# x read by channel and weight halves formed from the raw weights, in the opening of an RWKV + MoE layer

## Chip, core and metric

The kernel runs on one core of one Trainium2 chip. The metric is the device time of one execution in microseconds (us). The engines are TensorE (PE, with its weight loads PEld), VectorE (DVE), ScalarE (ACT), GpSimd (POOL) and SyncE (SP), which here only issues transfers.

## The reference

The layer works on x of 2 sequences x 2048 steps x 256 channels, in float32:

```python
xx = jnp.pad(x, ((0, 0), (1, 0), (0, 0)))[:, :-1, :]      # x one step earlier
xk = x * time_mix_k + xx * (1.0 - time_mix_k)             # the same for xv, xr
k, v, r = xk @ Wk.T, xv @ Wv.T, xr @ Wr.T
rwkv = sigmoid(r) * wkv(time_decay, time_first, k, v)     # a scan over the 2048 steps
x = _layernorm(x + rwkv @ Wo.T)
logits = x @ Wg + bg                                      # top 2 of 8 experts, softmax of the two
y_e = act_e(x @ W1[e] + b1[e]) @ W2[e] + b2[e]            # act: gelu for even e, silu for odd e
x = _layernorm(x + sum of the two chosen y_e, weighted)
```

## The kernel before

**Two phases.** Phase A computes the attention part and the routing, phase B the experts. In phase A the 2048 steps of both sequences are cut into 8 chunks of 256 (`NCH` = 8), each 512 columns wide (2 sequences) and 2 blocks of 128 channels deep (`CC` = 2). Phase B works through blocks of 256 tokens of one expert. Every engine has its own program, and they meet by semaphores. In each program phase A is a function `step(i)`, called for i from -2 to 9, in which the stages of several chunks stand in an order written out by hand. On VectorE step i begins with the running maximum of chunk i (`stabilise`: four scans at L1225, two `nd` operations at L1232), then come the division of chunk i-1 (`divide`), the two long scans q and p of chunk i (L1289, L1291, in `accumulate`), `numerator`, the residual of chunk i-1, its statistics, the routing of chunk i-2, and the lower halves of chunk i+2.

**Halves.** The projections are made from an upper and a lower half of each operand: the upper half is the value copied to the type fp32r, the lower is what is left. For x they are `xh` (ScalarE, L1023) and `xl` (VectorE, L1301), for the weights `wq`. x comes in by rows of time (`xin`), and TensorE turns it with eight 128x128 transposes to each chunk (`transpose_x`, L696) into `xT_ps`, from which both halves are read. Since a projection also needs x one step earlier, `xh` and `xl` have a column ahead of the chunk, which is copied from the chunk before (L1020, L1298).

**Projections.** `project` (L705) makes 24 products of 512 columns to each of k, v and r of a chunk. k of chunk i+1 waits for `nd` of chunk i (same PSUM banks). r and v share two banks: r of a chunk waits until v of the chunk before has been copied out, v waits until the sigmoid of r (`gates`, ScalarE L1000) has read them.

**Opening.** SyncE issues x of chunk 0, five small transfers with the mixing factors and decay constants as rows (`const_rows`), then Wk, Wv and Wr. TensorE first runs products of ones (`idle_products`, L677), turns the constants (L682), turns x, and runs more of them. Each weight matrix is multiplied by the mixing factor and by one minus it (`scale_matrix`, L417; Wk on VectorE, Wv and Wr on GpSimd) into `wscaled`; ScalarE copies the upper half in one operation (L970), VectorE takes the lower in one (L1151). Only then does k of chunk 0 start. b1 is also turned on TensorE (L687).

**ScalarE in step i.** Exponents of chunk i (L984 to L994), sigmoids of chunk i+1 (a table load at L1057 first), upper halves of chunk i+2, logarithm and exponential for the inverse of the denominator (`inverse`, L1029, L1031, with tables of their own), the normalisation (L1038), and the copy of v of chunk i+1 (`copy_v`, L979). In step 0 the second half of v of chunk 0 is copied behind the exponents.

**GpSimd** splits the first expert's weights, computes the reciprocal deviations and sends the routed rows to DRAM (L611). **SyncE** loads chunk i+2 of x when its transposes of chunk i are done.

## Time and profile before

| | us |
|---|---|
| median of 3 runs | 688.1 (687.56 to 694.36) |
| the profiled execution's own time | 694.94 |
| its span | 693.0 |
| mean granted TensorE clock | 0.954 of full speed |
| busy: PE | 629.8 (91%) |
| busy: DVE | 459.1 (66%) |
| busy: ACT | 378.3 (55%) |
| busy: POOL | 334.1 (48%) |

The span runs from the first to the last instruction on the core; the execution's time has 1.9 us more around it. The profiled execution is one of the longer ones. Phase A fills about the first 250 us, phase B reaches to about 660, the rest is the final normalisation. Shares over the whole span are averages over these stages, so the views below are taken by stage.

### The profile page before, as it was taken

To read this page: it belongs to the slowest core of one execution; us is meant where nothing else is said; L and a number is where in the kernel's file an instruction comes from. 1 tells how busy PE (TensorE), PEld (TensorE's weight loads), DVE (VectorE), ACT (ScalarE), POOL (GpSimd) and SP (SyncE) were. 2 spreads that over 40 slices of the span, in tenths; PEclk is the share of its full clock that TensorE was granted. 3 is DMA by queue.
4 is the path that set the end of the run, shared out by engine and by line. 5 is a ranking of instruction groups with operands and counts; after the bars stand their busy time and mean duration, and the time that the engine had idled before them with its cause. 6 is when DMAs were issued, how large, how long until landed. Compare 5 with 4: busy or idle time off the path is not lost.

```text
span 693.0 us, 14687 instructions
## 1 busy us (share of the span) xinstructions
PE 629.8 (91%) x4555; PEld 581.2 (84%) x4555; DVE 459.1 (66%) x1051; ACT 378.3 (55%) x690; POOL 334.1 (48%) x322
## 2 busy tenths in 40 slices
PE   7999999999977778999999999999999999999900
PEld 5787888878864567999999999999999999999900
DVE  4879999999998565555646465566575565555334
ACT  3566685585765223646463636375564646464417
POOL 6112037546546768229257374357384366131335
PEclk9999999999989789999999999999999999999965
DMA  8610221421324645532633525323516322331267
GB/s 245 169 32 0 92 92 63 138 85 54 108 92 152 223 156 150 160 58 38 175 47 124 94 46 154 64 49 119 96 29 177 55 42 42 53 46 17 35 197 309
DMA packets 53309, 70.61 MB, mean 102 GB/s; under 512 B 5482, under 2 KB 46900, under 8 KB 53076
## 3 DMA queue, kind: packets, MB, share of 16 engines
q1 hardware_dynamic: 31012, 43.24, 19.0%
q0 software_dynamic: 13216, 17.09, 14.0%
q10 hardware_dynamic: 8976, 8.82, 4.8%
q8 instruction: 73, 1.20, 0.7%
q14 instruction: 32, 0.26, 0.1%
HBM read 40.86 MB, written 29.06 MB: 101 GB/s over the span
## 4 chain that ended last, share of the span: by engine, by line
PE 71%; DVE 11%; issue 6%; ACT 5%; DMA 3%; POOL 2%; SPq 0%; DVEq 0%; ACTq 0%; POOLq 0%
PE y_ps L884 27%; PE hT_ps L875 26%; PE vr_ps L705 6%; PE k_ps L705 5%; ACT zz L1137 2%; PE xT_ps L893 2%; PE wo_ps L713 2%; DVE o_all L1225 2%; POOL records_dram L611 2%; PE small_ps L727 1%; DMA recs<-records_dram 1%; DVE xl L1301 1%; PE xT_ps L775 1%; PE xT_ps L696 1%; DVE nd L1232 1%
## 5 line engine op out<-in xcount | busy, mean ns | idle before, releaser
L875 PE MATMUL hT_ps<-xTh,wx 128*128 128x256 f32 x1120 | 208.2, 284 | 3.0 <-DVE aTl L1195 2.7
L649 POOL DMA_INDIRECT x_dram<-y_sb,dest x70 | 108.6, 1551 | 195.2 <-DVE y_sb L1212 117.7
L884 PE MATMUL y_ps<-wx,aTh 128*128 128x256 f32 x1088 | 190.9, 279 | 2.3 <-DVE y_sb L1212 2.3
L875 PEld LDWEIGHTS hT_ps<-xTh,wx 128*128 128x128 f32 x1120 | 175.5, 190 | 3.6 <-DVE aTl L1195 3.6
L1195 DVE TENSOR_TENSOR aTl<-hT_ps,aTh 128x512 fp32r<-128x512 f32 x140 | 93.5, 689 | 123.0 <-ACT aTh L1098 120.8
L884 PEld LDWEIGHTS y_ps<-wx,aTh 128*128 128x128 f32 x1088 | 165.4, 189 | 2.7 <-issue 2.7
L875 PE MATMUL hT_ps<-xTl,wx 128*128 128x256 f32 x560 | 157.3, 281 | 0.0
L884 PE MATMUL y_ps<-wx,aTl 128*128 128x256 f32 x544 | 151.7, 279 | 0.0
L1092 ACT ACT_TABLE_LOAD x33 | 42.3, 1283 | 161.4 <-PE hT_ps L875 159.8
L1092 ACT ACTIVATE hT_ps<-hT_ps,b_c 128x256 f32<-128x256 f32 x280 | 113.7, 469 | 23.7 <-PE hT_ps L875 21.1
L611 POOL DMA_INDIRECT records_dram<-rec,slot_i x64 | 77.4, 1209 | 64.7 <-DVE slot_i L1351 34.1
L875 PEld LDWEIGHTS hT_ps<-xTl,wx 128*128 128x128 f32 x560 | 106.5, 190 | 0.0
L884 PEld LDWEIGHTS y_ps<-wx,aTl 128*128 128x128 f32 x544 | 102.1, 188 | 0.0
L705 PE MATMUL vr_ps<-xh,wq 128*128 128x512 f32 x256 | 87.1, 412 | 0.1
L1098 ACT ACTIVATE aTh<-hT_ps 128x512 fp32r<-128x512 f32 x140 | 84.3, 648 | 0.0
L555 POOL TENSOR_TENSOR wx<-staging,wx 128x512 fp32r<-128x512 f32 x56 | 70.3, 1292 | 0.6
L705 PEld LDWEIGHTS vr_ps<-xh,wq 128*128 128x128 f32 x256 | 49.8, 195 | 12.1 <-ACT v L979 0.6
L1210 DVE TENSOR_TENSOR y_ps<-y_ps,b_b 128x256 f32<-128x256 f32 x70 | 30.1, 431 | 43.0 <-DVE weight L1191 19.6
L705 PE MATMUL vr_ps<-xl,wq 128*128 128x512 f32 x128 | 51.9, 405 | 0.0
L705 PE MATMUL k_ps<-xh,wq 128*128 128x512 f32 x128 | 42.3, 401 | 3.1 <-DVE nd L1232 2.1
L1212 DVE TENSOR_SCALAR y_sb<-y_ps,weight 128x256 f32<-128x256 f32 x70 | 33.9, 484 | 2.5
L705 PEld LDWEIGHTS k_ps<-xh,wq 128*128 128x128 f32 x128 | 24.2, 189 | 9.7 <-issue 4.1
(198 smaller groups left out, 845.3 us busy)
## 6 DMA issues: line engine op xcount, KB each, us to landing
staging<-in_L_ffn_W SPq DMA_DIRECT2D x16, 1024.0 KB
recs<-records_dram ACTq DMA_DIRECT2D x33, 261.0 KB, 3.4
xin<-in_L_attn_x SPq DMA_DIRECT2D x16, 256.0 KB, 4.3
xres<-in_L_attn_x SPq DMA_DIRECT2D x16, 256.0 KB, 3.2
x_dram<-rec SPq DMA_DIRECT2D x16, 256.0 KB, 3.4
zz<-x_dram SPq DMA_DIRECT2D x8, 512.0 KB, 7.6
out<-zz SPq DMA_DIRECT2D x8, 512.0 KB, 4.4
records_dram<-pad_rec SPq DMA_DIRECT2D x8, 261.0 KB, 3.9
```

The source lines that it names most:

```text
L555: pool.tensor_tensor(wx[:, e % 2, 1, at], raw[:, at], wx[:, e % 2, 0, at].bitcast(F32), ALU.subtract).then_inc(weights_ready if n == LOWER ...
L611: pool.indirect_dma_start(xs, bass.IndirectOffsetOnAxis(ap=slot_i[at][:, n:n + 1], axis=0), rec[at][:, j, :], None, bounds_check=DUMMY - 1 ...
L649: pool.indirect_dma_start(sums, bass.IndirectOffsetOnAxis(ap=dest[t.slot][:, h:h + 1], axis=0), y_sb[t.slot][:, h, :], None, bounds_check= ...
L705: ins = pe.matmul(out_ps.rearrange("p (b t) -> p b t", b=B), wq[:, mat, now, part, cc, oc * P:(oc + 1) * P], xpart[c.slot][:, cc, :, now:n ...
L713: ins = pe.matmul(wo_bank(c, b)[:, h, :], mixed[:, cc, b, h * P:(h + 1) * P], wo[:, cc, :], start=cc == 0, stop=cc == CC - 1)
L875: ins = pe.matmul(hT_ps[b][:, f, :], wx[:, s, part, off:off + P], xpart[t.slot % 2][:, cc, :], start=k == 0, stop=k == len(terms) - 1)
L884: ins = pe.matmul(y_ps[h], apart[t.slot % 2][:, fc, h * P:(h + 1) * P], wx[:, s, part, off:off + C], start=k == 0, stop=k == len(terms) - 1)
L1092: act.activation(hT_ps[b][:, f, :], hT_ps[b][:, f, :], func, bias=b1_c[:, bass.ds(expert * FC + (2 * b + f), 1)]).then_inc(act_done, 1)
L1098: act.activation(aTh[u.slot % 2][:, 2 * b - 2:2 * b, :], hT_ps[b - 1][:], ACT.Copy).then_inc(aTh_done, 1)
L1195: dve.tensor_tensor(aTl[u.slot % 2][:, 2 * b:2 * b + 2, :], hT_ps[b][:], aTh[u.slot % 2][:, 2 * b:2 * b + 2, :].bitcast(F32), ALU.subtract ...
L1210: dve.tensor_tensor(y_ps[h], y_ps[h], b2_b[:, bass.ds(expert * C, C)], ALU.add).then_inc(bias_added, 1)
L1212: dve.tensor_scalar(y_sb[u.slot][:, h, :], y_ps[h], weight[u.slot][:, h:h + 1], None, ALU.mult).then_inc(y_done, 1)
```

## The change

**Layouts.** x is also handed over with channels as rows (`x_by_channel`), the mixing factors, decay and first as one 128x10 array of columns, b1 as 128x64 columns. These arrays exist before the launch. `xt` takes the place of `xin`; the transposes of x, of the constants and of b1 fall away. Each load of `xt` brings the column of one step earlier with it (257 columns), so the two small copies fall away, and from chunk 1 on each half of x is one operation of 128x1028 (in chunk 0 one to each channel block).

**Weights' halves.** ScalarE forms the upper half straight from the raw weights, four operations of 128x256 to each matrix with the factor as the per-partition scale; VectorE forms the lower with `scalar_tensor_tensor`, four to each matrix. `scale_matrix` falls away.

**Order.** x of chunk 0 is issued on ScalarE's own queue. TensorE begins with 16 products of ones in a row. In step 0 ScalarE copies v before the exponents, and takes the upper halves of chunk 2 and the inverse ahead of the sigmoids of chunk 1, with two more table loads.

```diff
+        def load_turned(sp, c):
+            skip = 1 if c.number == 0 else 0
+            for b in range(B):
+                sp.dma_start(xt[c.slot][:, :, b, skip:TC + 1],
+                             xT[b].rearrange("(c p) t -> p c t", p=P)[:, :, c.number * TC - 1 + skip:(c.number + 1) * TC]).then_inc(xt_in[c.slot], 16)
...
-            load_chunk(sp, xin[0], x, plain(0), xin_in[0])
-            for n, row in enumerate([m.rearrange("a b (c p) -> (a b c) p", p=P) for m in (mix_k, mix_v, mix_r)] +
-                                    [v.rearrange("(c p) -> c p", p=P) for v in (decay, first)]):
-                sp.dma_start(const_rows[n * CC:(n + 1) * CC, :], row).then_inc(consts_in, 16)
+            sp.dma_start(consts_c[:], columns).then_inc(consts_in, 16)
             load_matrix(0, wkT)
             load_matrix(1, wvT)
             load_matrix(2, wrT)
+            load_turned(sp, plain(1))
...
-                    sp.wait_ge(xT_done, (c - 2).upto(CC))
-                    load_chunk(sp, xin[c.slot], x, c, xin_in[c.slot])
+                    sp.wait_ge(xl_done, (c - 2).upto(1))
+                    load_turned(sp, c)
...
-            idle_products(6, vr_ps[0][:])
-            pe.wait_ge(consts_in, 5 * 16)
-            pe.transpose(small_ps[:, 256:256 + 5 * CC], const_rows[:], ident[0:5 * CC, 0:5 * CC]).then_inc(consts_turned, 1)
+            idle_products(16, vr_ps[0][:])
...
+                    if c.number == 0 and mat == 0 and oc == 0 and n % (len(terms) // CC) == 0:
+                        pe.wait_ge(w_lo, 2 * (cc + 1))
+                        pe.wait_ge(*((first_xl, cc + 1) if cc < CC - 1 else (xl_done, 1)))
...
-                    if (i + 2).exists:
-                        transpose_x(i + 2)
...
             def upper_weights(n):
-                act.wait_ge(scaled[n], 2 * CC)
-                act.activation(wq[:, n, :, 0, :, :], wscaled_of(n), ACT.Copy).then_inc(w_hi, 1)
+                if n == 0:
+                    act.wait_ge(setup_dve, 1)
+                act.wait_ge(weights_in[n], 16)
+                for cc, a, factor in parts():
+                    act.activation(wq[:, n, a, 0, cc, :], raw_matrix(n, cc), ACT.Identity,
+                                   scale=factor[:, n, cc:cc + 1]).then_inc(w_hi, 1)
...
                 if i.exists:
-                    exponents(i)
                     if i.number == 0:
                         copy_v(i, 1)
+                    exponents(i)
...
-                if (i + 1).exists and i.number >= 0:
+                if i.number == 0:
+                    upper_halves(i + 2)
+                    inverse(i)
+                    act.preload_act_table(ACT.Sigmoid)
                     gates(i + 1)
-                    act.preload_act_table(ACT.Ln)
-                if (i + 2).exists and i.number >= 0:
-                    upper_halves(i + 2)
-                if i.exists:
+                    act.preload_act_table(ACT.Exp)
+                elif i.exists:
+                    if (i + 1).exists:
+                        gates(i + 1)
+                        act.preload_act_table(ACT.Ln)
+                    if (i + 2).exists:
+                        upper_halves(i + 2)
                     inverse(i)
...
             def lower_halves(c):
...
+                rows = lambda a: a[:].rearrange("p c b t -> p (c b) t")[:, :, 0:TC + 1]
+                dve.tensor_tensor(rows(xl[c.slot]), rows(xt[c.slot]), rows(xh[c.slot]).bitcast(F32), ALU.subtract).then_inc(xl_done, 1)
```

ScalarE, from the first instruction to v of chunk 0. Before:

```order
L966 ACT_TABLE_LOAD
L966 ACTIVATE consts_c<-consts_c 128x2
L970 ACTIVATE wq<-num 128x2x512
L1023 ACTIVATE xh<-xT_ps 128x2x256 x2
L970 ACTIVATE wq<-den 128x2x512
L970 ACTIVATE wq<-r 128x2x512
L1020 ACTIVATE xh<-xh 128x4
L1023 ACTIVATE xh<-xT_ps 128x2x256 x2
L979 ACTIVATE v<-vr_ps 128x512
```

And with the change (`nd` is where Wk lies at first):

```order
L378 DMA xt<-in_x_by_channel 128x2x256 x2
L936 ACT_TABLE_LOAD
L936 ACTIVATE consts_c<-consts_c 128x2
L943 ACTIVATE wq<-nd,unmix_c 128x256
L943 ACTIVATE wq<-nd,consts_c 128x256
L943 ACTIVATE wq<-nd,unmix_c 128x256
L943 ACTIVATE wq<-nd,consts_c 128x256
L996 ACTIVATE xh<-xt 128x2x257 x2
```

The one long copy is now four short operations on the raw matrix, and the engine also issues the loads of x. The eight operations for Wv and Wr follow behind `xh`.

ScalarE in step 0, from the exponents of chunk 0 to the copy of v of chunk 1. Before:

```order
L989 ACTIVATE A<-A 128x4x256
L979 ACTIVATE v<-vr_ps 128x512
L994 ACTIVATE bonus<-nd,consts_c 128x512 x2
L1057 ACT_TABLE_LOAD
L1000 ACTIVATE gate<-vr_ps 128x512 x4
L1064 ACT_TABLE_LOAD
L1020 ACTIVATE xh<-xh 128x4
L1023 ACTIVATE xh<-xT_ps 128x2x256 x2
L1029 ACTIVATE r<-den 128x1024
L1031 ACT_TABLE_LOAD
L1031 ACTIVATE r<-r 128x1024
L979 ACTIVATE v<-vr_ps 128x512 x2
```

And with the change:

```order
L963 ACTIVATE A<-A 128x4x256
L968 ACTIVATE bonus<-nd,consts_c 128x512 x2
L1033 ACT_TABLE_LOAD
L974 ACTIVATE gate<-vr_ps 128x512 x2
L999 ACTIVATE xh<-xt 128x4x257
L1005 ACT_TABLE_LOAD
L1005 ACTIVATE r<-den 128x1024
L1007 ACT_TABLE_LOAD
L1007 ACTIVATE r<-r 128x1024
L1042 ACT_TABLE_LOAD
L974 ACTIVATE gate<-vr_ps 128x512 x2
L1044 ACT_TABLE_LOAD
```

The sigmoids of chunk 1 (the third and fourth `gate`) moved behind the inverse of chunk 0, between two table loads that were not there.

TensorE at the start. Before:

```order
L677 MATMUL vr_ps<-ones_h 128x512 x6
L682 MATMUL small_ps<-ident,const_rows 128x10
L696 MATMUL xT_ps<-ident,xin 128x128 x8
L677 MATMUL vr_ps<-ones_h 128x512 x4
L687 MATMUL small_ps<-ident,b_rows 128x64
L677 MATMUL vr_ps<-ones_h 128x512 x5
```

And with the change:

```order
L667 MATMUL vr_ps<-ones_h 128x512 x16
L681 MATMUL k_ps<-xh,wq 128x512
L681 MATMUL k_ps<-xl,wq 128x512
L681 MATMUL k_ps<-xh,wq 128x512 x2
L681 MATMUL k_ps<-xl,wq 128x512
```

Fifteen products of ones with transposes between them became sixteen in a row.

## Rows read from the trace of the kernel before

**Rows 1.** Windows by stage: times, busy us (instructions) by engine, PEclk, DMA share, GB/s

```profile
115.00:117.00 2.00, 2.00 (x6) 1.51 (x6) 1.90 (x8) 1.98 (x3) 1.74 (x4) 0.50 0.32 115
117.30:143.20 25.90, 25.90 (x136) 21.41 (x135) 24.96 (x56) 16.78 (x26) 14.42 (x17) 1.00 0.31 103
193.60:265.60 72.00, 51.92 (x308) 41.19 (x307) 52.36 (x169) 31.14 (x55) 44.00 (x48) 0.81 0.47 155
265.60:660.00 394.40, 389.98 (x3348) 388.98 (x3347) 222.78 (x473) 208.80 (x433) 199.47 (x132) 1.00 0.38 80
```

**Rows 2.** Chain of waits that ended last: start us, us, what

```profile
3.40 2.77 DMA nd<-in_L_attn_Wk
69.68 5.88 PE k_ps L705 x24
83.79 1.73 PE wo_ps L713 x8
87.73 0.94 PE xT_ps L696 x8
103.34 5.67 PE vr_ps L705 x24
113.89 7.18 PE vr_ps L705 x24
169.19 1.44 DVE o_all L1225 x3
```

**Rows 3.** Timeline of TensorE, opening: start us, us, engine, line, operation, count [idle before]

```profile
2.46 2.74 PE L677 MATMUL vr_ps<-ones_h 128*128 128x512 bf16 x6 [2.46 <-POOL lane L534]
7.09 1.60 PE L677 MATMUL vr_ps<-ones_h 128*128 128x512 bf16 x4
8.83 1.25 PE L677 MATMUL vr_ps<-ones_h 128*128 128x512 bf16 x5
11.10 0.47 PE L705 MATMUL k_ps<-xh,wq 128*128 128x512 f32 x1 [1.02 <-DVE xl L1301]
```

**Rows 4.** Transfers of the first 12 us: KB each, median us to landing

```profile
xin<-in_L_attn_x SPq DMA_DIRECT2D x4, 256.0 KB, 3.2
```

**Rows 5.** Timeline of ScalarE, phase A

```profile
18.04 1.07 ACT L1023 ACTIVATE xh<-xT_ps 128x512 fp32r<-128x512 f32 x2
44.96 1.28 ACT L1031 ACT_TABLE_LOAD   x1
46.25 1.06 ACT L1031 ACTIVATE r<-r 128x1024 f32<-128x1024 f32 x1
47.22 1.07 ACT L979 ACTIVATE v<-vr_ps 128x512 f32<-128x512 f32 x2
93.10 2.06 ACT L1038 ACTIVATE rec<-xres,shift,rstd 128x256 f32<-128x256 f32 x4
```

**Rows 6.** Timeline of VectorE, phase A

```profile
26.57 1.23 DVE L1285 TENSOR_TENSOR b2v<-B,v 128x1024 f32<-128x1024 f32 x1 [3.23 <-ACT v L979]
47.34 1.23 DVE L1246 TENSOR_TENSOR newton<-den,r 128x1024 f32<-128x1024 f32 x1 [1.96 <-ACT r L1031]
52.35 2.29 DVE L1289 TENSOR_TENSOR_SCAN q_all<-A,B 128x1028 f32<-128x1028 f32 x1
66.23 2.66 DVE L1225 TENSOR_TENSOR_SCAN o_all<-w_row,o_all,k_ps 128x256 f32<-128x256 f32 x4
91.39 2.66 DVE L1225 TENSOR_TENSOR_SCAN o_all<-w_row,o_all,k_ps 128x256 f32<-128x256 f32 x4
111.35 0.68 DVE L1363 TENSOR_TENSOR xres<-wo_ps,xres 128x512 f32<-128x512 f32 x1
115.49 0.17 DVE L1298 CAST xl<-xl 128x4 fp32r<-128x4 f32 x1
115.57 1.28 DVE L1301 TENSOR_TENSOR xl<-xT_ps,xh 128x512 fp32r<-128x512 f32 x2
117.23 2.66 DVE L1225 TENSOR_TENSOR_SCAN o_all<-w_row,o_all,k_ps 128x256 f32<-128x256 f32 x4 [0.30 <-DVE o_all L1220]
```

More of the change, by code:

```diff
@@ L81, in upto, with build @@
         return self.m * (self.every * each) + (self.off * each + n)
-def build(nc, x, decay, first, mix_k, mix_v, mix_r, wkT, wvT, wrT, woT, w1, b1, w2, b2, wgT, bg, out):
+def build(nc, x, wkT, wvT, wrT, woT, w1, w2, b2, wgT, bg, xT, columns, b1_columns, out):
     B, T, C = x.shape
@@ L193, in build @@
         rec = [sb(f"rec{n}", [P, J, REC], F32, phase_a) for n in range(RECS)]
-        xin = [sb(f"xin{n}", [P, B, TH, C], F32, phase_a) for n in range(2)]
+        xt = [sb(f"xt{n}", [P, CC, B, TC + 2], F32, phase_a) for n in range(2)]
         xres = [sb(f"xres{n}", [P, B, TH, C], F32, phase_a) for n in range(2)]
@@ L1141, in _ @@
         def _(dve):
[L1142 to L1144 removed]
+            dve.wait_ge(consts_in, 16)
             dve.tensor_scalar(unmix_c[:], mix_c, -1.0, 1.0, ALU.mult, ALU.add).then_inc(setup_dve, 1)
[L1146 to L1147 removed]
+            dve.memset(A2[:, :, :, 0:1], 0.0).then_inc(setup_dve, 1)
+            dve.memset(seen[:], 0.0).then_inc(setup_dve, 1)
+            dve.wait_ge(setup_act, 1)
+            dve.tensor_scalar(decay_c, decay_c, -1.0, None, ALU.mult).then_inc(setup_dve, 1)
+            dve.wait_ge(setup_dve, 4)
+            dve.tensor_tensor(first_c, first_c, decay_c, ALU.add).then_inc(setup_dve, 1)
+            for cc in range(CC):
+                dve.tensor_copy(w_row[:, cc, :], decay_c[:, cc:cc + 1].broadcast_to([P, TC])).then_inc(setup_dve, 1)
             def lower_weights(n):
[L1150 to L1153 removed]
+                for part, (cc, a, factor) in enumerate(parts()):
+                    dve.wait_ge(w_hi, 2 * CC * n + part + 1)
+                    dve.scalar_tensor_tensor(out=wq[:, n, a, 1, cc, :], in0=raw_matrix(n, cc), scalar=factor[:, n, cc:cc + 1],
+                                             in1=wq[:, n, a, 0, cc, :].bitcast(F32), op0=ALU.mult, op1=ALU.subtract).then_inc(w_lo, 1)
             def finish_setup():
@@ L1157, in finish_setup @@
                 lower_weights(2)
[L1158 to L1166 removed]
+                dve.wait_ge(setup_dve, 5 + CC)
                 dve.wait_ge(made2, 9)
[L1168 to L1169 removed]
             def halves(u):
@@ L1498 @@
     arrays, aps = {}, []
-    for name in INPUTS:
-        a = np.asarray(inputs[name])
-        a = np.ascontiguousarray(a.T if name in TRANSPOSED else a)
+    given = {name: np.asarray(a) for name, a in inputs.items()}
+    laid_out = {name: given[name].T if name in TRANSPOSED else given[name] for name in INPUTS}
+    laid_out["x_by_channel"] = given["L0_attn_x"].transpose(0, 2, 1)
+    laid_out["columns"] = np.concatenate([given[name].reshape(-1, P) for name in COLUMNS]).T
+    laid_out["b1_columns"] = given["L0_ffn_b1"].reshape(-1, P).T
+    for name, a in laid_out.items():
+        a = np.ascontiguousarray(a)
         arrays[f"in_{name}"] = a
```

130 lines of the change are left out of this document (41 added, 89 removed).

## The prediction

> **What bounds the kernel now.** I read the windows by stage first, then the chain of waits, then the timelines of TensorE, ScalarE and VectorE in phase A. Phase B is TensorE alone, busy 389.98 of 394.40 us [rows 1]; the change puts nothing there and takes nothing away, so I cost it at nothing. In phase A two engines are almost equally full: in the window from 117.30 TensorE is busy for all of its 25.90 us and VectorE for 24.96 [rows 1]. So work taken from TensorE alone pays only as far as VectorE allows. The opening is a serial chain that nothing hides: the landing of Wk (issued at 3.40, landed at 6.17 [rows 2]), scaling, upper and lower half, halves of x, and k of chunk 0 at 11.10, with TensorE idle for 1.02 us before it [rows 3].
>
> The sum below is made against the profiled execution, span 693.0 and own time 694.94 us. That is 6.8 us above the median of 688.1; two of the four executions known lie near 694 and two near 688.
>
> **Opening (until k of chunk 0).** SyncE no longer issues x and five small transfers ahead of Wk, only the columns, so Wk is issued at about 1.2 in place of 3.40. At its old landing time of 2.77 it would be there at 4.0 [rows 2]. It now shares the transfer engines with x of chunk 0, issued on the other queue at 0.8; a 256 KB transfer of x took 3.2 in the median [rows 4]. I take 4.4 for Wk and 5.3 for x. ScalarE then makes four upper halves of 128x256 in place of one copy. The nearest row is four operations of that size in 2.06 [rows 5], so they end at 6.5; the two upper halves of x take 1.07 [rows 5], and half of that, then one lower half of 128x514 on VectorE (1.28 for two [rows 6]) gives 6.5 + 0.55 + 0.65 + small gaps = 7.8. The four lower halves of Wk run one behind ScalarE's and are done by 7.0. The halves of Wv and Wr (eight more operations, some 4.2 us on ScalarE by the same row) end at about 11.7, behind k's 5.9 us, so they are hidden; without that cover they would cost up to 2.1 to each matrix.
>
> But TensorE's 16 products of ones stand ahead of k. At the low of the two clock levels six of them took 2.74, 0.43 each from the second on, and later, at the high one, five took 1.25 [rows 3]. From 2.46 all sixteen at 1.2 GHz last until 9.3. In the execution before, four products from 7.09 still took 1.60, the five from 8.83 were fast [rows 3]; with a rise at about 8.6 here too they end at 9.0. If the clock rises three us earlier, they end at about 7.4, and the data at 7.8 decide. No row shows which. I take 8.4, the middle. **Opening: 11.10 - 8.4 = 2.7 us, between 1.8 and 3.3.**
>
> **Steps 0 and 1.** k, v and r take 5.6 to 5.9 us each (k 5.88, r 5.67 [rows 2]). From k of chunk 0 TensorE works without a pause until v of chunk 1, whose copy at 47.22 releases ScalarE's exponents [rows 5] and these the scan q at 52.35 [rows 6]. Two groups of eight transposes stood in that stretch, 0.94 each by the chain's piece at 87.73 [rows 2]: 1.9 us. For this to count, VectorE and ScalarE must keep up. Today VectorE waits 3.23 us for v of chunk 0 at 26.57 and 1.96 for the inverse at 47.34 [rows 6]. The first wait shrinks: v is copied ahead of the exponents. In its place b2v waits for the exponents themselves, which start when v's second half is out (8.4 + 5.9 + 5.7 + 0.6 for the copy = 20.6) and are ready three operations of about 1.0 later, at 23.6, 2.97 before today's 26.57. The second goes: the inverse is ready at about 34 (worked out below), and VectorE, which reached it at 45.4 and waited [rows 6], reaches the division at about 39. What is late next is the copy of v of chunk 1, as before: v ends at 47.2 - 2.7 - 1.9 = 42.6, and q starts at about 47.7 in place of 52.35. VectorE then idles some 3.6 us ahead of b2v, off the path. The larger halves `xh` of chunk 1 to 7 cost no more than today's two pieces (1.07). Behind q, the product with the gate meets the sigmoid of chunk 2 about 0.2 late. **Steps 0 and 1: 1.9 - 0.2 = 1.7 us.** The first scan of step 2, at 66.23 before, comes at about 61.8.
>
> The moved order adds two table loads to ScalarE's step 0. A load took 1.28, and the exponential behind it began 1.29 after the load did [rows 5]. So inverse and sigmoids of chunk 1 line up as: `xh` 29.4, load and logarithm 31.7, load and exponential 34.1, load 35.4, first sigmoid 36.0. TensorE wants to start v of chunk 1 at 37.1 and finds its bank free: the loads lie in the shadow of r. The Trainium skill, ScalarE: Activation LUTs, section What ACT_TABLE_LOAD costs, speaks against this: each switch of set costs a drain of about 1.38 us on top of the load. The trace does not agree, since nothing of that length stands behind the load in the rows. By that page the first sigmoid would end three drains later, and the sum would be smaller by the amount given among the rivals.
>
> **Steps 2 to 5.** Each loses its eight transposes on TensorE (0.94), one small copy on each of ScalarE and VectorE, and two lower halves become one. VectorE sets the pace now. Step 3 lasts 117.23 - 91.39 = 25.84 us and holds 0.30 of waiting [rows 6]; the rest, 25.54, is VectorE's own. The small copy goes (the next operation starts 0.08 after it), and one operation of 128x1028 in place of two (1.28 [rows 6]) should take as long as b2v's 128x1024, 1.23 [rows 6]: 25.4 remain. Step 2 (25.16) has no waiting for x, and wins only 0.13. Step 3 wins 0.43, and steps 4 and 5, 169.19 - 117.23 = 51.96 [rows 2, 6], win 1.15. In step 6 no halves are made, and it stays. **Steps 2 to 5: 1.7 us.** TensorE's other 0.6 us a step turn into idle time before k. Bounds: 0.5, if the waits above VectorE's own pace came only from the low clock in this execution (a window at 0.50 [rows 1], v of a chunk 7.18 in place of 5.67 [rows 2]); 2.5, if VectorE's small gaps close too.
>
> **What costs nothing.** GpSimd loses `scale_matrix` in the opening; its next work waits for the first expert's weights anyway. SyncE's loads of x now wait for VectorE's lower halves of two chunks back and come many us early. b1 comes in as it is used. The rest of phase A and the tail are only shifted.
>
> **Sum.** 2.7 + 1.7 + 1.7 = 6.1 us of 694.94 gives 688.8 for an execution like the profiled one. Against the median of 688.1 I take off 5.6, since part of the 1.7 in steps 2 to 5 is what the low clock cost there: **682.5 us**, 0.8% less.
>
> **The rivals.**
> - *The spread of the runs.* Executions near 694 and near 688 both occur, and the stretch from 193.60 to 265.60 has a granted clock of 0.81 [rows 1], so its length can vary. If the new median is one of the longer ones: 694.6 - 6.1 = 688.5. Two of the four executions known speak for it; against it, two of the three runs that make the median before were short.
> - *The opening is given back.* x by channel is read in pieces 8 KB apart. If they land 3 us late, k starts at 10.8 and the gain is 5.6 - 2.4: 684.9. Against it: every transfer of that piece length lands in about 3 us [rows 4]. If also the first clock rise is late, no more is lost, since it lies beside.
> - *Table loads with a drain.* Three drains end the first sigmoid of chunk 1 at 40.1, 3.0 after TensorE wants v: 682.5 + 3.0 = 685.5. This is the page's rule as a mechanism; the rows speak against it.
> - *More than the sum.* If the transposes also caused the low clock in steps 3 and 5, and the later start of the tail falls well, up to 4 us more come: 678.5. For it: the slow v follows directly on the routing products and the transposes.
> - *Slower.* TensorE now stands idle before every k from step 2 on, 1.3 to 1.7 us a step. If that brings its clock down for k and what follows until the second half of the out-projection, the chain that ends at 83.79 + 1.73 [rows 2], this lies on VectorE's path: the residual there is due at 111.35, 19.96 us into its step, and the chain takes 85.52 - 66.23 = 19.29 [rows 2, 6], slack 0.67. One stretch at the low clock costs 7.18 - 5.67 = 1.5 [rows 2], two a step 3.0, less the slack 2.3, over four steps 9.3: 682.5 + 9.3 = 691.8, slower than before. It decides from 2.1 us of lost time a step. Against it: an idle of 1.02 before k in the opening is followed by k products at full pace.
>
> **Chances.** Forecast 0.52 (its own range 679.5 to 685), spread 0.14, opening given back 0.09, drains 0.03, more than the sum 0.15, slower 0.07. That the change does not do what it says is not open here. About 1% is what a measurement can tell from no change, 681.2 and 695.0. Of the forecast's case about 0.4 lies below 681.2, since the bounds of the opening (0.6) and of the steps (0.8) both leave room there; with the case of more, faster is 0.52 x 0.4 + 0.15 = 0.36. Slower by over 1% needs the low clock before k and the longer runs together: 0.04. Same: 0.60. The range of 678.5 to 689 leaves out 0.2, the slower case and edges of others.
>
> **What would show it.** k of chunk 0 starting at 7.8 to 9.3; scan q of chunk 1 at about 47.7; steps 2 to 5 of 25.0, then 25.4 us; TensorE idle for over 1 us before each k; no idle on TensorE before v of chunk 1. A start of k after 10, a wait of v of chunk 1 for `gates`, or steps above 25.8 would make the prediction wrong.

## The result and the profile after

The changed kernel takes 687.28 us in the median of 20 runs (683.97 to 689.82), the kernel before 691.94 in the median of 20 (687.56 to 694.97): ratio 0.9936, 95% interval 0.9919 to 0.9953. The medians are 4.7 us apart; by the ratio the gain is 4.4 us (3.3 to 5.6). Forecast were 682.5 us and, against the 688.1 shown then, 5.6 us less, a ratio of 0.9919. The profiled execution of the changed kernel has a span of 688.0 and an own time of 689.71, where the one before had 693.0 and 694.94.

The windows by stage of the changed kernel, which answer to [rows 1] (step 3 starts 5.5 us earlier here, and its low clock lies elsewhere in the step); the columns are as there:

```profile
115.00:117.00 2.00, 1.81 (x8) 1.53 (x9) 1.97 (x4) 1.27 (x2) 0.00 (x0) 1.00 0.91 305
111.70:137.20 25.50, 24.67 (x121) 20.11 (x120) 24.81 (x55) 17.52 (x24) 14.78 (x15) 0.94 0.32 104
187.00:265.60 78.60, 61.47 (x359) 49.62 (x358) 56.35 (x176) 33.01 (x59) 50.04 (x53) 0.78 0.50 162
265.60:655.00 389.40, 384.15 (x3297) 383.31 (x3295) 220.08 (x466) 206.80 (x429) 194.09 (x128) 1.00 0.38 78
```

VectorE is now busy for 24.81 of a step of 25.50 us, and TensorE for 24.67, with pauses of its own. Next the chain of waits (start us, us, what), for [rows 2]:

```profile
2.45 6.34 PE vr_ps L667 x16
8.79 5.68 PE k_ps L681 x24
48.39 1.73 PE wo_ps L689 x8
82.92 7.27 PE vr_ps L681 x24
98.77 5.69 PE vr_ps L681 x24
162.69 1.44 DVE o_all L1203 x3
```

The chain now opens with the sixteen products of ones (`vr_ps L667`) in place of the landing of Wk. One v still takes 7.27 us where others take 5.7. The timeline of TensorE, for [rows 3], and its waits before a later k (in brackets the idle time and what ended it):

```profile
2.45 6.34 PE L667 MATMUL vr_ps<-ones_h 128*128 128x512 bf16 x16 [2.45 <-POOL lane L528]
8.56 0.47 PE L681 MATMUL k_ps<-xh,wq 128*128 128x512 f32 x1
64.89 0.47 PE L681 MATMUL k_ps<-xh,wq 128*128 128x512 f32 x1 [1.70 <-DVE nd L1210]
115.19 0.47 PE L681 MATMUL k_ps<-xh,wq 128*128 128x512 f32 x1 [0.83 <-DVE nd L1210]
166.14 0.47 PE L681 MATMUL k_ps<-xh,wq 128*128 128x512 f32 x1 [1.37 <-DVE nd L1210]
```

k of chunk 0 starts at 8.56 in place of 11.10. Transfers of the first 12 us (KB each, median us to landing), for [rows 4]:

```profile
xt<-in_x_by_channel ACTq DMA_DIRECT2D x2, 256.0 KB, 4.3
nd<-in_L_attn_Wk SPq DMA_DIRECT2D x1, 256.0 KB, 4.1
```

ScalarE, for [rows 5]: the last of the four upper halves of Wk, the first of the exponents of chunk 0, then inverse and sigmoid in their new order, and the second copy of v of chunk 1:

```profile
6.67 0.49 ACT L943 ACTIVATE wq<-nd,consts_c 128x256 fp32r<-128x256 f32 x1
20.68 1.05 ACT L958 ACTIVATE B<-nd 128x1024 f32<-128x1024 f32 x1
29.17 1.28 ACT L1005 ACT_TABLE_LOAD   x1
30.46 1.06 ACT L1005 ACTIVATE r<-den 128x1024 f32<-128x1024 f32 x1
31.55 1.28 ACT L1007 ACT_TABLE_LOAD   x1
32.84 1.06 ACT L1007 ACTIVATE r<-r 128x1024 f32<-128x1024 f32 x1
33.92 1.28 ACT L1042 ACT_TABLE_LOAD   x1
35.21 0.60 ACT L974 ACTIVATE gate<-vr_ps 128x512 f32<-128x512 f32 x1
42.75 0.60 ACT L953 ACTIVATE v<-vr_ps 128x512 f32<-128x512 f32 x1 [2.22 <-PE vr_ps L681]
```

VectorE, for [rows 6]: the lower halves of x of chunk 0, `b2v` and q of chunk 1, the single lower half of a chunk, and the first scans of steps 2 to 7:

```profile
7.72 1.30 DVE L1275 TENSOR_TENSOR xl<-xt,xh 128x514 fp32r<-128x514 f32 x2
46.22 1.23 DVE L1263 TENSOR_TENSOR b2v<-B,v 128x1024 f32<-128x1024 f32 x1 [3.06 <-ACT B L961]
47.36 2.30 DVE L1267 TENSOR_TENSOR_SCAN q_all<-A,B 128x1028 f32<-128x1028 f32 x1
61.45 2.66 DVE L1203 TENSOR_TENSOR_SCAN o_all<-w_row,o_all,k_ps 128x256 f32<-128x256 f32 x4
86.25 2.66 DVE L1203 TENSOR_TENSOR_SCAN o_all<-w_row,o_all,k_ps 128x256 f32<-128x256 f32 x4
110.39 1.23 DVE L1281 TENSOR_TENSOR xl<-xt,xh 128x1028 fp32r<-128x1028 f32 x1
111.74 2.66 DVE L1203 TENSOR_TENSOR_SCAN o_all<-w_row,o_all,k_ps 128x256 f32<-128x256 f32 x4
137.21 2.66 DVE L1203 TENSOR_TENSOR_SCAN o_all<-w_row,o_all,k_ps 128x256 f32<-128x256 f32 x4
162.69 2.66 DVE L1203 TENSOR_TENSOR_SCAN o_all<-w_row,o_all,k_ps 128x256 f32<-128x256 f32 x4
187.06 2.66 DVE L1203 TENSOR_TENSOR_SCAN o_all<-w_row,o_all,k_ps 128x256 f32<-128x256 f32 x4
```

The steps last 24.8, then 25.49, 25.47, 25.48 and 24.37 us. Behind phase A lies phase B, which begins with the first product of hT. The timeline of TensorE shows it at 248.11 in the kernel before and at 241.75 in the changed one, 6.36 us earlier:

```profile
248.11 0.55 PE L875 MATMUL hT_ps<-xTh,wx 128*128 128x256 f32 x1
```
```profile
241.75 0.55 PE L844 MATMUL hT_ps<-xTh,wx 128*128 128x256 f32 x1
```

The last stage begins with the last scatter of results. The chain of waits there, in the kernel before and in the changed one:

```profile
660.87 3.64 DMA x_dram<-y_sb,dest
665.63 3.65 DMA zz<-x_dram
672.99 12.90 ACT zz L1137 x26
```
```profile
654.15 3.61 DMA x_dram<-y_sb,dest
658.88 5.38 DMA zz<-x_dram
667.98 12.39 ACT zz L1121 x25
```

From the last scatter to the end the kernel before takes 693.0 - 660.87 = 32.1 us, the changed one 688.0 - 654.15 = 33.8. The first eighth of the rows lands 3.65 us after its issue in the one, 5.38 in the other.

The account of the two profiled executions: start of step 7, 193.58 to 187.06, 6.52 less; from there to phase B 54.53 and 54.69; phase B to the last scatter 412.76 and 412.40; last stage 1.72 more. 6.52 - 0.16 + 0.36 - 1.72 = 5.0, the difference of the spans. Single profiles of one kernel differ too (the kernel before starts step 7 between 192.56 and 193.58 in its three profiles), so this account is repeated below with means of three.

### The profile page after: what moved, and what is told of

Read it like the earlier page. It is cut to its first block, busy times and chain, and to the rows that moved or that the text cites. A ratio compares the mean times of both kernels' runs of the same rounds, so it can differ in the third digit from the quotient of the medians.

```text
span 688.0 us, 14522 instructions
## 1 busy us (share of the span) xinstructions
PE 626.3 (91%) x4490; PEld 576.9 (84%) x4490; DVE 458.8 (67%) x1040; ACT 382.7 (56%) x687; POOL 330.3 (48%) x313
## 3 DMA queue, kind: packets, MB, share of 16 engines
HBM read 40.88 MB, written 29.06 MB: 102 GB/s over the span
## 4 chain that ended last, share of the span: by engine, by line
PE 72%; DVE 12%; issue 6%; ACT 3%; DMA 3%; POOL 3%; DVEq 0%; ACTq 0%; SPq 0%; POOLq 0%
PE hT_ps L844 27%; PE y_ps L853 27%; PE vr_ps L681 7%; PE k_ps L681 4%; ACT zz L1121 2%; PE xT_ps L862 2%; POOL records_dram L601 2%; DVE o_all L1203 2%; PE wo_ps L689 1%; DMA recs<-records_dram 1%; DVE stats L1300 1%; PE vr_ps L667 1%; PE small_ps L703 1%; DMA zz<-x_dram 1%; DVE newton L1231 1%
## 5 line engine op out<-in xcount | busy, mean ns | idle before, releaser
L601 POOL DMA_INDIRECT records_dram<-rec,slot_i x64 | 75.1, 1174 | 65.7 <-DVE slot_i L1330 34.8
L689 PE MATMUL wo_ps<-wo,newton 128*128 128x256 f32 x112 | 29.5, 411 | 4.2 <-DVE newton L1231 4.2
```

What stands on the lines that cost most here:

```text
L601: pool.indirect_dma_start(xs, bass.IndirectOffsetOnAxis(ap=slot_i[at][:, n:n + 1], axis=0), rec[at][:, j, :], None, bounds_check=DUMMY - 1 ...
L689: ins = pe.matmul(wo_bank(c, b)[:, h, :], mixed[:, cc, b, h * P:(h + 1) * P], wo[:, cc, :], start=cc == 0, stop=cc == CC - 1)
```

## The experiments

Each kernel was run several times beside the kernel before on the same chip; four chips served in these runs, on which the kernel before has medians of 692.0, 694.2 (693.9 in a second group of runs), 696.3 and 697.7 us. Ratios are to the kernel before, with 95% intervals. Three questions stand behind them: which part of the change gives what in phase A; where the rest of the forecast is; and what TensorE's clock does in the tail of phase A, the stretch from step 7 to hT. The letters that the expectations give to their theories are explained there. This table has all runs (starts in us, from each profile; "last stage" is from the last scatter to the end):

| run | ratio | k of chunk 0 | q of chunk 1 | step 7 | hT | last stage |
|---|---|---|---|---|---|---|
| kernel before | | 11.10 | 52.35 | 193.58 | 248.11 | 32.1 |
| before again (2nd) | 1.0009 (0.9986 to 1.0031) | 11.14 | 52.02 | 192.56 | 246.83 | 31.3 |
| before again (3rd) | 0.9998 (0.9974 to 1.0021) | 11.15 | 52.02 | 193.10 | 248.34 | 31.9 |
| changed | 0.9936 (0.9919 to 0.9953) | 8.56 | 47.36 | 187.06 | 241.75 | 33.8 |
| changed again (2nd) | 0.9938 (0.9911 to 0.9964) | 8.30 | 47.10 | 186.82 | 241.07 | 33.8 |
| changed again (3rd) | 0.9928 (0.9904 to 0.9953) | 8.38 | 47.30 | 187.01 | 242.96 | 32.9 |
| step 0 in the old order | 0.9943 (0.9917 to 0.9969) | 8.46 | 48.90 | 188.16 | 242.0 | 33.3 |
| before, x by channel only | 1.0018 (0.9998 to 1.0037) | 11.29 | 51.97 | 191.22 | 245.49 | 33.2 |
| before, second copy unused | 0.9985 (0.9967 to 1.0003) | 11.12 | 51.99 | 193.15 | 248.18 | 32.5 |
| changed, copy declared last | 0.9929 (0.9902 to 0.9956) | 7.71 | 46.51 | 186.23 | 242.16 | 33.2 |
| changed, transposes back | 0.9928 (0.9904 to 0.9952) | 7.93 | 48.48 | 189.10 | 244.07 | 33.5 |
| changed, gate on GpSimd | 0.9925 (0.9899 to 0.9952) | 8.43 | 47.34 | 185.95 | 241.34 | 33.7 |
| changed, spare rows | 0.9928 (0.9904 to 0.9953) | 8.01 | 46.81 | 186.51 | 240.63 | 33.8 |
| before, spare rows | 1.0005 (0.9982 to 1.0027) | 11.06 | 51.95 | 192.44 | 246.54 | 31.6 |
| changed, 8 idle products | 0.9868 (0.9835 to 0.9900) | 8.48 | 47.28 | 186.97 | 238.22 | 33.0 |
| before, 8 idle products | 0.9955 (0.9934 to 0.9976) | 11.15 | 52.35 | 193.90 | 244.66 | 33.4 |
| changed, opening late | 0.9956 (0.9934 to 0.9979) | 11.71 | 50.63 | 190.35 | 246.51 | 33.7 |
| changed, 14 idle products | 0.9930 (0.9906 to 0.9954) | 8.29 | 47.08 | 186.83 | 245.20 | 33.1 |
| changed, 8 again | 0.9941 (0.9916 to 0.9965) | 8.53 | 47.33 | 187.08 | 241.64 | 34.8 |
| changed, 4 idle products | 0.9935 (0.9910 to 0.9960) | 8.56 | 47.48 | 187.21 | 243.77 | 35.1 |

### Both kernels again

> The kernel before, unchanged, profiled a second time. Theory T (phase A gained what was forecast, and the rest of the program gave some back by chance): its step 7 begins between 192.0 and 193.6 us, and from there to the last scatter of phase B it differs from the first profile's 467.3 us by up to 3 us either way. Theory L (the first profile was a lucky or unlucky one in phase A): its step 7 begins more than 1.5 us away from 193.6. Time: same as before, 692 us within 1.

> The changed kernel, unchanged, profiled a second time. Theory T: k of chunk 0 starts at 8.4 to 9.0, step 7 at 187.1 within 0.8; the final stage, from the last scatter on, takes 32.1 us as in the kernel before and not 33.9 again. Theory P (the second copy of x in memory slows the last loads and stores): the final stage takes 33.9 again. Time 687.3 within 1.

The gain repeats: 0.9938 after 0.9936, and 1.0009 for the kernel before against itself. So a ratio of this size is resolved, and differences of a quarter of a per cent between two edited kernels are not. Step 7 of the kernel before starts at 192.56, as theory T has it. The last stage of the changed kernel takes 33.8 us again, which theory P expected and theory T did not.

### Step 0 in the old order

```diff
+                    exponents(i)
                     if i.number == 0:
                         copy_v(i, 1)
-                    exponents(i)
...
-                if i.number == 0:
-                    upper_halves(i + 2)
-                    inverse(i)
-                    act.preload_act_table(ACT.Sigmoid)
-                    gates(i + 1)
-                    act.preload_act_table(ACT.Exp)
```

> The changed kernel with ScalarE's old order in step 0: the exponents before the copy of v, the sigmoids of chunk 1 before the upper halves and the inverse, two table loads fewer. If the order matters as in the forecast (VectorE waited for the inverse), scan q of chunk 1 comes later by up to 1 us, since VectorE would reach the division at 39 and the inverse be ready at about 42: the division ends at about 46.5, b2v's partner is ready at 46.2, so 0.3 to 1.5 us slower. Rival (the order is idle, PE's chain through v of chunk 1 sets q anyway): no change within 0.5 us.

q of chunk 1 starts at 48.90, 1.5 to 1.8 us later than in the changed kernel's three profiles, and step 7 1.1 to 1.3 later. ScalarE then comes to the copies of v too late, as its timeline in this kernel shows (43.77 for both, behind the inverse, where the changed kernel copied the second half at 42.75):

```profile
41.51 1.28 ACT L1007 ACT_TABLE_LOAD   x1
42.80 1.06 ACT L1007 ACTIVATE r<-r 128x1024 f32<-128x1024 f32 x1
43.77 1.07 ACT L953 ACTIVATE v<-vr_ps 128x512 f32<-128x512 f32 x2
```

So the moved order is worth a good microsecond in the profile; in the timed runs 0.9943 against 0.9938 shows no difference, and intervals of half a per cent could not show one of that size.

### Before, with x by channel only

```diff
-            load_chunk(sp, xin[0], x, plain(0), xin_in[0])
+            load_turned(sp, plain(0))
...
-                    transpose_x(i + 2)
-                    idle_products(4, vr_ps[0][:])
+                    idle_products(8, vr_ps[0][:])
```

> The kernel before with x by channel alone: no transposes of x, constants and weights as before, k of chunk 0 about where it was, at 11. Theory of the forecast: it gains the 1.7 us of steps 0 and 1 less what the old order in step 0 keeps (0 to 1), and the 1.1 to 1.7 of steps 2 to 5, so step 7 begins 2 to 3.4 us before 193.6 and the time is 688.5 to 690. Rival (the opening is all of the gain): step 7 begins within 1 us of the kernel before and the time is 691 to 692.

The ratio is 1.0018 (0.9998 to 1.0037), where 2 to 3.5 us less were expected: this part alone wins nothing that the time shows. k of chunk 0 waits for its data as before (the timeline of TensorE), because the scaling of Wk still stands ahead of it:

```profile
11.29 0.47 PE L701 MATMUL k_ps<-xh,wq 128*128 128x512 f32 x1 [1.14 <-DVE xl L1291]
```

q of chunk 1 stays at 51.97 although sixteen transposes are gone: without the new order VectorE and ScalarE hold it. Only steps 2 to 6 shorten, 191.22 - 65.61 = 125.61 against 193.58 - 66.23 = 127.35 (126.67 and 127.21 in the two other profiles of the kernel before, so by 1.1 to 1.7), and the last stage is longer by 1 to 2 us. Step 7 comes 1.3 to 2.4 us earlier than in those three profiles, and none of it arrives in the time.

### The second copy of x in memory

In the kernel before, x by channel is declared and 4 KB of it read; in the changed kernel, it is declared behind the output.

```diff
+            sp.dma_start(spare[:], xT[0, 0:P, 0:8]).then_inc(spare_in, 16)
```
```diff
+    result = nc.dram_tensor("out", shape, F32, kind="ExternalOutput").ap()
```

> The kernel before, with x by channel handed over as a further array that is not used (one 4 KB read of it in the opening, no engine waits for it). Theory P (the mere presence of a further 4 MB array moves what the final stage reads, and makes that slower): the first load of the final stage takes 4.9 to 6.7 us in place of 3.6, the stretch from the last scatter to the end 33.2 to 33.9 in place of 31.3 to 32.1, and the time rises by about 1.7 us over the kernel before. Rival (what the kernel reads matters, not what lies there): 3.6, 31.3 to 32.1, and the same time.

> The changed kernel with x by channel declared behind the output array. Theory P, if the order of declaration decides where the arrays lie: the first load of the final stage takes 3.6 us again, the final stage 31.3 to 32.1, and the time is 1.7 us below the changed kernel. If it does not decide: no change. Rival: no change.

0.9985 and 0.9929: neither the presence of the array nor its place in the list shows a cost in time. The last stages are 32.5 and 33.2 us. That the place in the list moves the array in memory isn't shown, so theory P gets no support here, but is not excluded either. In the profile with the unused copy the chain waits for a load that landed 6.92 us after its issue, although nothing is read by channel but 4 KB: such late landings are not the changed kernel's alone.

### The transposes' work put back

```diff
+                        for j in range(J):
+                            pe.transpose(xT_ps[:, cc, j * P:(j + 1) * P], ident[:], ident[:])
```

> The changed kernel with eight transposes of the identity where the transposes of x stood (none of them waited for, in the opening one group behind k of chunk 0). Theory of the forecast (TensorE's share was worth 1.7 us in steps 0 and 1 and, since VectorE then sets the pace, 1.1 to 1.7 in steps 2 to 5): step 7 begins at about 190 in place of 187, scan q of chunk 1 at 49.1, steps 3 to 5 take 25.7 to 25.9, and the time rises by 3 us. Rival (steps 2 to 5 are VectorE's alone): steps 3 to 5 stay at 25.5 and step 7 begins at 189.

k of chunk 0 starts at 7.93 and q of chunk 1 at 48.48, 40.55 apart, where the changed kernel has 38.80 and the kernel before 41.25 (40.88 and 40.87 in its other profiles). Put back, the two groups of transposes cost 1.75 us in steps 0 and 1. Put beside the run with x by channel only, 51.97 - 11.29 = 40.68, this shows that neither part does it alone: the transposes taken out win 0.2 to 0.6 us here, the new order 0.3 to 0.7, both together 2.0 to 2.5. Steps 2 to 6 take 189.10 - 62.57 = 126.53 against 125.61, so 0.9 there. The timed ratio, 0.9928, doesn't show these 2.7 us (0.4%), where 3 us were expected. Its interval is half a per cent wide; the six runs lie between 687.71 and 690.74 us, those of the changed kernel with the copy declared last between 687.14 and 691.20.

### The gate's product on GpSimd

```diff
-                dve.tensor_tensor(num[:], num[:], gate[i.slot][:], ALU.mult).then_inc(gated_done, 1)
+                    pool.tensor_tensor(num[:], num[:], gate[i.slot][:], ALU.mult).then_inc(gated_done, 1)
```

> The changed kernel with the product with the gate (1.14 us of VectorE's path in each chunk) moved to GpSimd. Theory (VectorE is the bound in steps 2 to 6): these steps shorten, each until TensorE's about 24.7, so by 0.7 to 1.1 us, step 7 begins 4 to 6 us earlier and the time falls by as much. Rival (TensorE or the chain through both engines still bounds): steps stay at 25.5. Third way: GpSimd is slower on it than VectorE's slack (2.6 us or more) or slows VectorE on the same memory port, and the division waits: steps longer than 25.5.

1.2 us taken from VectorE in each step bring step 7 forward by only 1.1 us (185.95), where 4 to 6 were expected; all of it is won in steps 2 to 6, since step 2 starts at 61.43 as before. These steps take 24.8, 25.8, 24.8, 25.4 and 23.7. Only steps 4 and 6 are shorter than in the changed kernel (25.5 and 24.4 there), and in both TensorE had pauses: in windows at their bounds it was busy for 24.64 and 23.00 us. In steps 3 and 5 of the changed kernel it was busy for all of the 25.5 us, VectorE for 24.8, and there less work on VectorE wins nothing. Both engines are nearly full, as the prediction read it in [rows 1].

### The place of the row results in memory

```diff
-    xs = nc.dram_tensor("records_dram", (DUMMY + BLK, REC), F32, kind="Internal").ap()
+    xs = nc.dram_tensor("records_dram", (DUMMY + BLK + B * T, REC), F32, kind="Internal").ap()
```

> The changed kernel, with 4 MB of unused rows added to the records' array in device memory, so that the array of row results behind it may lie elsewhere; no instruction changes. So far the stage from the last scatter to the end took 33.2 to 33.9 us in every kernel that reads x by channel, and 31.3 to 32.5 us in three profiles of kernels that don't. If the place of the row results in memory sets that (theory A), this kernel's last stage moves, to 31.3 to 32.5 us, and the time drops by about 1.5 us against the changed kernel (ratio to the kernel before 0.991). If it is something that the change does to the last stage itself, or the change's own arrays do by being read (theory B), it stays at 33.2 to 33.9 us (ratio 0.993). Phase A as in the changed kernel in both: first scan of step 7 at 186.5 to 187.5 us.

> The kernel before, with the same 4 MB of unused rows added to the records' array. Theory A (place in memory): the last stage may move to 33.2 to 33.9 us, and the time rises by about 1.5 us (ratio 1.002). Theory B: it stays at 31.3 to 32.5 us (ratio 1.000). If it comes to over 33 us here although nothing is read by channel, theory B falls; if both kernels with the spare rows stay as they are, theory A falls. Phase A as before: first scan of step 7 at 192.5 to 193.6 us.

Neither kernel's last stage moves: 33.8 and 31.6 us. Nothing supports theory A, though no row shows that the array of row results did move.

### The opening made late

```diff
-            idle_products(16, vr_ps[0][:])
+            idle_products(32, vr_ps[0][:])
```

> The changed kernel with 32 idle products in the opening instead of 16, so that the first k product comes at 14.6 to 14.9 us instead of 8.5 and every later step of phase A about 6.2 us later, at the times of the kernel before. If a microsecond of phase A is a microsecond of the whole (theory E), the time rises by 6.2 us against the changed kernel (ratio to the kernel before 1.0015 to 1.003), and the last stage stays at 33.2 to 33.9 us. If the last stage and the stretch behind the last scan step are shorter when everything is later (theory F: the kernel before gets back there what it lost), the last stage falls to 31.3 to 32.5 us and the ratio comes to 0.999 to 1.000.

The dose was half of what I had worked out: the sixteen more took 9.62 - 6.34 = 3.3 us, 0.21 each, as the timeline of TensorE in this kernel shows.

```profile
2.45 9.62 PE L667 MATMUL vr_ps<-ones_h 128*128 128x512 bf16 x32 [2.45 <-POOL lane L528]
11.71 0.58 PE L681 MATMUL k_ps<-xh,wq 128*128 128x512 f32 x1
```

k of chunk 0 and step 7 both come 3.3 us later than in the third profile of the changed kernel on the same chip (11.71 and 8.38; 190.35 and 187.01). The medians are 694.32 and 691.11, 3.2 us apart; the ratios 0.9956 and 0.9928 make it 2.0, with intervals that overlap. This fits theory E, a microsecond of the whole for each microsecond of the opening, but does not measure it closely. The last stage doesn't get shorter (33.7), so with this dose nothing is seen of theory F.

### A third profile of both, for the last stage

> The kernel before once more, for its last stage: 32.13 and 31.27 us in its two profiles so far. If the difference of the last stage between the two kernels is real, it comes to 31.2 to 32.5 us again (ratio 1.000); if it is chance, it may as well come to over 33 us, as in the kernel before with idle products (33.35 us).

> The changed kernel once more, for its last stage: 33.85 and 33.84 us in its two profiles so far, with the first load landing 5.4 us after its issue. Real difference: 33.2 to 33.9 us again; chance: anything from 31.3 us on. Ratio to the kernel before 0.993 to 0.994; phase A as in its other profiles (first scan of step 7 at 186.8 to 187.1 us).

Ratios 0.9998 and 0.9928. The load that the last stage waits for, in the chains of the kernel before (the first load) and of the changed one (here the second, issued 0.4 us behind the first):

```profile
666.32 3.50 DMA zz<-x_dram
```
```profile
660.06 6.21 DMA zz<-x_dram
```

Last stages of 31.9 and 32.9 us, the second below the 33.2 that a real difference was expected to give. In this profile of the changed kernel the first load was not late: VectorE starts on its rows at 663.52, 3.9 us after its issue. Over three profiles each the kernel before has 32.1, 31.3 and 31.9, the changed one 33.8, 33.8 and 32.9. The two don't overlap, and the mean difference is 1.8 us; of the edited kernels before, those with x by channel and with idle products have 33.2 and 33.4.

### Idle products in the tail of phase A

```diff
                             turn_early(0)
+                            idle_products(8, k_ps[:, 1, :])
```

> The changed kernel, with 8 idle products more in each step behind the last scan step, where the granted clock fell to half in its profile (226.8 to 247.3 us). If the clock in the tail of phase A is what TensorE's work there waits for (theory C: it also sets the spread of the runs, 684 us at a mean clock of 0.956 and 690 at 0.947), the clock stays high, the tail from the first scan of step 7 to the first y product drops from 77.3 to 79.3 us by 3 to 6 us, and the ratio to the kernel before comes to 0.985 to 0.990. If the products only add work (theory D), the tail is 1 to 3 us longer and the ratio 0.994 to 0.998.

> The kernel before, with the same 8 idle products in each step behind the last scan step. Its tail took 78.1 to 79.2 us in three profiles. Theory C (the clock in the tail decides): 3 to 6 us less, ratio 0.991 to 0.996, as much as for the changed kernel, since the tail is the same work in both. Theory D: ratio 1.001 to 1.004. If the products help one kernel and not the other, the tail isn't the same in both, and the forecast's part that the rest is only shifted fails there as well.

> The candidate for the best version, with two edits: 14 idle products instead of 8 behind the first turned half in each step behind the last scan step, and 12 instead of 16 in the opening. Theory C (TensorE's granted clock in the tail decides): the clock stays high through more of the tail, the ratio to the kernel before comes to 0.980 to 0.986. If 8 were enough already, or more of them only stand in front of the work, 0.987 to 0.991. The opening gives at most 0.7 us (first k product at 7.7 to 8.4 us, set by the data).

> The changed kernel with 8 idle products more in each step behind the last scan step, once more. Their first run gave 0.987 against the kernel before, 0.7% better than the changed kernel; 14 of them gave 0.993, no better than it. If 8 are right and 14 too many (theory C with a price: each costs its 0.21 us in front of the work), this run gives 0.985 to 0.989, and the first hT product comes at 238 to 240 us with a granted clock above 0.9 from 236 us on. If the first run was chance, the ratio comes to 0.991 to 0.995 and the first hT product at 241 to 243 us.

> The same with 4 idle products. Theory C with a price: half of the effect or all of it (0.985 to 0.991), since 4 cost only 0.8 us in front of the work of each step. If only the sum of work in the right place counts, and 8 was chance, 0.992 to 0.995 as in the changed kernel.

On the first chip 8 products helped both kernels: 0.9868, where the changed kernel with spare rows had 0.9928 on the same chip, and 0.9955 for the kernel before. hT began at 238.22. Windows of that run (times, busy us by engine, PEclk, DMA share, GB/s), then of its repeat on another chip, show what differs:

```profile
236.00:252.00 16.00, 13.42 (x107) 11.82 (x106) 12.75 (x48) 9.08 (x21) 10.86 (x12) 0.93 0.47 171
```
```profile
224.00:232.00 8.00, 5.59 (x32) 3.52 (x33) 4.56 (x29) 2.80 (x7) 5.64 (x9) 0.59 0.37 130
232.00:240.00 8.00, 4.58 (x37) 3.03 (x35) 3.88 (x24) 0.77 (x3) 6.05 (x7) 1.00 0.87 269
240.00:248.00 8.00, 6.58 (x35) 6.58 (x36) 4.88 (x20) 2.96 (x6) 4.09 (x4) 0.57 0.40 135
```

In the repeat the same program has the low level, 1.2 GHz, through much of 240 to 248, hT starts at 241.64, and the ratio is 0.9941. With 14 it is 0.9930, hT as late as 245.20 (that run has a second edit, 12 products in the opening in place of 16); with 4 it is 0.9935. The low stretch of the changed kernel's own profile is this window,

```profile
226.80:247.30 20.50, 17.17 (x81) 14.01 (x81) 11.51 (x57) 5.69 (x11) 12.99 (x18) 0.51 0.55 175
```

and in it the sixteen small products of the routing take 3.58 us where they take 1.95 at the high level. So the clock has a price in the tail. But it doesn't set the start of hT by itself, as TensorE's timeline in the run with 14 products shows:

```profile
236.59 1.95 PE L703 MATMUL small_ps<-wg,x1T 128*128 128x8 f32 x16
244.22 0.21 PE L776 MATMUL small_ps<-picks,before_h 128*128 128x32 bf16 x1 [4.36 <-DVE picks L1251]
```

Here the routing products run at the high level and end at 238.5, and then VectorE, which has nothing else to do, starts the first operation on their result only at 242.39, after an idle of 4.51 us for which the profile names no engine ("remote"). Such idles of 1 to 4.5 us, ahead of this operation or of the one that reads the counts made from it (`rank`), stand in the tail of the repeat with 8 products (1.24, 2.59 and 1.85), of the run with 4 (2.66 and 3.34), of the third profile of the changed kernel (2.12 and 3.39) and of all three of the kernel before; in the one good run with 8, and in the first two profiles of the changed kernel, there is none. What causes them is open. So for theory C a price of the clock is shown, on these products, but not what it is worth in the whole. As a remedy the idle products fail: they did not bring the gain a second time. No version was shown to be faster than the changed kernel on more than one chip.

## Why the prediction was right and wrong

**What failed: the level, first.** The step that failed is the base of the sum: "Against the median of 688.1 I take off 5.6". That median came from 3 runs, and two of the four executions known lay near 694. Over 20 runs the kernel before has 691.94. This base is 3.84 of the 4.78 us between 682.5 and 687.28. For an execution like the profiled one the same sum gave 688.8, and the profiled execution of the changed kernel took 689.71. The rival "the spread of the runs", at 0.14, gave this mechanism; it put the base at 694.6 and the time at 688.5, too high by 1.2. The measured ratio is safe from this, since both kernels were run side by side.

**What failed second: "the rest of phase A and the tail are only shifted."** The last stage was put at nothing and takes 1.8 us more (31.8 and 33.5 in the means of three profiles each). Up to hT the sentence held: step 7 comes 6.1 us earlier (193.08 and 186.96), and the way from there to hT takes 54.7 and 55.0. Phase B up to the last scatter takes 413.0 and 411.8; it was costed at nothing too, and gives 1.2 back, about as much as two profiles of the changed kernel differ (1.3). Together, 6.1 - 0.3 + 1.2 - 1.8 = 5.3 us in the profiles, forecast 6.1; 4.4 in the timed runs, forecast 5.6. In the last stage SyncE issues the same eight loads of 512 KB, and ScalarE's 32 operations take 15.8 us in both; what differs is how late the load on the chain lands. None of the experiments shows a cause: not the second copy's presence or its place in the list, not the added rows ahead of the row results, not an opening that starts 3.3 us later. Reading x by channel is not needed for a long last stage either: the kernel before with 8 idle products has 33.4 us. The cause stays open.

**What the timed runs do not show.** The shares below are read from profiles. Of the timed gain, only the opening's share has support from timed runs (3.2 us in the medians for 3.3 of delay). Taking out the transposes alone gave 1.0018, and putting their work back left 0.9928. So that the gain in steps 0 to 5 arrives in the time is argued from the account of the spans, not shown.

**Opening: right, in part by luck.** Forecast 8.4 (2.7 us), measured 8.56, 8.3 and 8.38, 2.7 in the mean. The parts differ: Wk and x took 4.1 and 4.3 us to land, and Wk, forecast for 4.4, let ScalarE start on its halves only at 5.46. The lower half of x's first block was there at about 7.72 + 0.65 = 8.4, not 7.8, and the products of ones ended beside it. 8.4 was the middle between two cases. In the second profile the products of ones took 5.07 us and ended at 7.5, and TensorE waited 0.79 us for the lower half; in the first and third they took 6.3 and TensorE did not wait.

**Steps 0 and 1: right, a little too low.** q of chunk 1 was forecast at 47.7 and came at 47.36; step 2 at 61.8, and came at 61.45: 2.2 us instead of 1.7 (1.9 in the means of three). The predicted new idle ahead of `b2v` is there, 3.06 us (forecast 3.6), ended by the exponents and not by v. The forecast did not give the moved order a price: with the old one, 1.5 of it is lost at q.

**Table loads: right.** Each load took 1.28 us, and the operation behind it began 1.29 after the load did, three times in a row (29.17 to 30.46, 31.55 to 32.84, 33.92 to 35.21). The first sigmoid started at 35.21, forecast 36.0. By the Trainium skill, ScalarE: Activation LUTs, What ACT_TABLE_LOAD costs, about 1.38 us of drain come on top of each load. This trace shows none, behind a load or ahead of it (the logarithm ends at 31.52, the next load starts at 31.55), and that rival is out.

**Steps 2 to 5: right.** 102.96 us in the kernel before, 101.24 now, 1.7 less as forecast, and 1.5 in the means of three; steps 3 to 5 take 25.5 (forecast 25.4), and the single lower half 1.23. Step 6 stays at 24.4.

**The other rivals.** *Given back in the opening*: out, k starts at 8.3 to 8.6. *More than the sum*: out; a v of 7.27 us is still there without the transposes of x, so they are not needed for the low clock. *Slower*: out; after idles of 1.70, 0.83 and 1.37 us k runs at full pace. The sign given for the forecast, TensorE idle for over 1 us before each k, was half wrong: it idles before k in only three of the steps. In steps 3 and 5 a v at the low clock right before it had used up the pause (granted clock 0.57 in both of the windows 82.92 to 86.90 and 134 to 138).

## What to carry to other kernels

Take the level of the kernel before from many runs, or forecast the ratio: with a spread of 1% between executions, the median of three was off by 3.8 us, nearly as much as the whole change. When one engine is relieved in a kernel where two are full, look for the order of work on the others that lets the time through; here either part alone won at most 0.7 us in steps 0 and 1, and both together 2.0 to 2.5. And read the stages behind the change in both profiles, however far off: 1.8 us of 6.1 went in the last one, and 1.2 came back in phase B.

## What the runs showed of the hardware

- The same program on four chips, each at its own time, has medians from 692.0 to 697.7 us. This difference, 0.8%, is larger than the change; the ratio carries over (0.9936, 0.9938 and 0.9928).
- Eight loads of 512 KB from device memory, issued back to back, took SyncE 3.9 to 5.4 us to issue in the kernel before and 4.8 to 5.3 in the changed one, and the one on the chain landed 3.5 to 3.7 us after its issue in the one, 5.4 to 6.2 in the other. In the edited kernels before the one on the chain, not always the first, took from 3.33 to 7.36 us.
- A product of ones of 512 columns took 0.21 us at the high clock level: sixteen of them added in the opening moved k of chunk 0 and step 7 by 3.3 us each.
- VectorE sat idle for 1 to 4.5 us ahead of the routing operations in the tail, with no engine named as the cause, in some executions of a program and not in others (2.12 and 3.39 us in the third profile of the changed kernel, none in the first two).
- ScalarE's 128x256 operations with one pointer as scale follow each other at 0.40 us (6.27, 6.67), closer than the 0.51 that rows with two pointers gave.
